# Computing elu+1 with two VectorE operations and one ScalarE operation, and storing and reloading the output accumulator block by block, in a linear-attention and mixture-of-experts kernel

## The reference

```python
x = x + attn(layernorm(x))
x = x + ffn(layernorm(x))

# attn: 16 heads of 64, linear attention
q = elu(q) + 1.0
k = elu(k) + 1.0
kv = einsum('bhnd,bhne->bhde', k, v)
out = einsum('bhnd,bhde->bhne', q, kv) / (q . sum(k) + 1e-8)
out = out @ w_proj + b_proj

# ffn: 8 experts of width 2048, gates by three Sinkhorn rounds, top 2 of 8
g = relu(x @ wg[e]); p = x @ wp[e]
all_out = (g * p) @ wo[e]
return x + sum over the two chosen experts of gate * all_out
```

## Time and profile before

| | us |
|---|---|
| median of 3 timed runs | 8018.8 |
| the three runs | 7903.87, 8018.8, 8377.97 |
| the profiled execution, call | 7267.14 |
| the profiled execution, span of its slowest core | 7265.5 |
| spans of the 8 cores | 7255.6 to 7265.5 |

### The profile page before, as it was taken

How to read it: one execution, slowest core, us unless ns; L and a number is a source line. 1 busy time by engine, 2 the same in 40 slices (tenths; PEclk the granted TensorE clock), 3 DMA queues, 4 the chain that set the end, 5 groups by cost and what they waited for, 6 DMA issues and landing times.

```text
span 7265.5 us, 77246 instructions; the slowest of 8 cores (7255.6 to 7265.5 us)
## 1 busy us (share of the span) xinstructions
PE 6219.6 (86%) x28666; PEld 2747.6 (38%) x29238; DVE 2713.8 (37%) x4957; ACT 977.8 (13%) x1646; POOL 165.5 (2%) x202
## 2 busy tenths in 40 slices
PE   4666655569999999999999996999999999999998
PEld 1222222224444444444444442444444444444443
DVE  2222244443433333333343332333334333333333
ACT  2323311111111111111111110111111111111110
POOL 0000000000000000000000000000000000000000
PEclk8888866679999999999999998999999999999999
DMA  4000011132222222222222224222222222222222
GB/s 73 21 24 18 21 55 55 56 87 35 35 35 35 35 35 40 41 42 36 35 35 35 35 35 110 41 40 42 35 35 35 35 35 35 35 35 35 35 38 62
DMA packets 192672, 298.65 MB, mean 41 GB/s; under 512 B 5930, under 2 KB 137002, under 8 KB 192306
## 3 DMA queue, kind: packets, MB, share of 16 engines
q0 software_dynamic: 169120, 209.75, 19.8%
q1 hardware_dynamic: 23186, 83.93, 3.5%
HBM read 469.84 MB, written 33.55 MB: 69 GB/s over the span
## 4 chain that ended last, share of the span: by engine, by line
PE 68%; DVE 13%; issue 9%; ACT 7%; DMA 2%; DVEq 0%; SPq 0%; ACTq 0%; POOL 0%; POOLq 0%
PE p3p L714 24%; PE p3g L709 24%; PE p3o L754 13%; DVE out_acc L769 8%; PE p1kv L321 2%; PE p2pr L501 2%; ACT rt L726 2%; DVE kb L339 1%; DMA rws<-router_w 1%; PE p2tr L438 1%; ACT qtmp L336 1%; ACT qtmp L384 1%; DVE h2T L442 1%; DVE h1T L309 1%; ACT h1b L296 1%
## 5 line engine op out<-in xcount | busy, mean ns | idle before, releaser
L754 PE MATMUL p3o<-wo_p,t 128*128 128x512 bf16 x8031 | 1841.6, 379 | 333.5 <-DVE out_acc L769 325.5
L709 PE MATMUL p3g<-h2T,wg_p 128*128 128x512 bf16 x8028 | 1923.1, 379 | 9.2 <-DVE sk L628 0.5
L714 PE MATMUL p3p<-h2T,wp_p 128*128 128x512 bf16 x8025 | 1921.6, 379 | 9.0 <-issue 0.2
L736 DVE TENSOR_TENSOR t<-rt,p3p 128x512 bf16<-128x512 f32 x1024 | 704.8, 688 | 3021.3 <-ACT rt L726 3021.2
L769 DVE SCALAR_TENSOR_TENSOR out_acc<-p3o,wsel,out_acc 128x512 f32<-128x512 f32 x2048 | 1482.3, 748 | 483.0 <-PE p3o L754 335.1
L754 PEld LDWEIGHTS p3o<-wo_p,t 128*128 128x128 bf16 x8192 | 783.6, 98 | 1351.5 <-issue 446.1
L726 ACT ACTIVATE rt<-p3g 128x512 f32<-128x512 f32 x1024 | 611.3, 597 | 5047.5 <-PE p3p L714 5047.5
L709 PEld LDWEIGHTS p3g<-h2T,wg_p 128*128 128x128 bf16 x8192 | 802.2, 98 | 968.9 <-issue 7.2
L714 PEld LDWEIGHTS p3p<-h2T,wp_p 128*128 128x128 bf16 x8192 | 802.1, 98 | 968.3 <-issue 5.5
L321 PE MATMUL p1kv<-wqkv_sb,h1T 128*128 128x512 bf16 x992 | 290.4, 442 | 67.6 <-DVE kb L339 39.3
L305 PE MATMUL p1tr<-identb_s,h1b 128*128 128x128 bf16 x256 | 53.4, 262 | 171.5 <-ACT h1b L296 139.5
(11 more groups left out here) (118 smaller groups left out, 1354.8 us busy)
## 6 DMA issues: line engine op xcount, KB each, us to landing
wg_p<-wg POOLq DMA_DIRECT2D x64, 1024.0 KB, 11.3
wp_p<-wp POOLq DMA_DIRECT2D x64, 1024.0 KB, 17.3
wo_p<-wo POOLq DMA_DIRECT2D x64, 1024.0 KB, 21.9
xt<-x SPq DMA_DIRECT2D x64, 512.0 KB, 3.6
base_scr<-xt SPq DMA_DIRECT2D x32, 512.0 KB, 2.6
out_acc<-base_scr SPq DMA_DIRECT2D x32, 512.0 KB, 15.1
out<-out_acc SPq DMA_DIRECT2D x32, 512.0 KB, 7.5
wqkv_sb<-w_qkv POOLq DMA_DIRECT2D x1, 6144.0 KB, 43.2
```

The costliest lines, as they stand in the source:

```text
L709: EM(T, lambda t, b=b, k=k, fsub=fsub, w=w, q=q, it3=it3: t.matmul(p3g[it3 % 2][:], wg_sb[b][:, 512 * k + 128 * fsub:512 * k + 128 * (fsub ...
L714: mmfn = lambda t, b=b, k=k, fsub=fsub, w=w, q=q, it3=it3: t.matmul(p3p[it3 % 2][:], wp_sb[b][:, 512 * k + 128 * fsub:512 * k + 128 * (fsu ...
L736: EM(V, lambda v, qt=qt, fsub=fsub, it3=it3: v.tensor_tensor(t_sb[qt][:, 512 * fsub:512 * (fsub + 1)], rt_sb[it3 % 2][:], p3p[it3 % 2][:], ...
L754: mmfn = lambda t, qt=qt, s4=s4, fsub=fsub, b=b, dmh=dmh: t.matmul(p3o[s4][:], t_sb[qt][:, 512 * fsub + 128 * s4:512 * fsub + 128 * (s4 + 1)],
```

## The change

Three things:

- elu+1 in stage 1, for keys and queries: VectorE writes min(y, 0) from PSUM to `qtmp1` or `qtmp2` in turn, ScalarE takes Exp of it into `qtmp3`, and VectorE computes max(y, 0) + `qtmp3` from PSUM in one operation. VectorE now waits for the matmuls and for the Exp before, ScalarE for the minimum.
- The 16 loads of wave 0 stay ahead of stage 3. Every output block has its own point in the count of additions (`su_done`), noted when the second half of its last addition is emitted. SyncE waits for that point and stores the block.
- In wave 0 it then waits until this store has landed and issues the load of the same block for wave 1. In wave 1 it goes on to the next block.

```diff
             if cc < 2:
-                W(S, SM["kv"])
+                W(V, SM["kv"])
+                W(V, SM["sks"])
+                EM(V, lambda v, pb=pb, cc=cc: v.tensor_single_scalar(
+                    qtmp1[:] if cc == 0 else qtmp2[:], pb[:], 0.0, ALU.min).then_inc(SM["skv"].h, 1))
+                inc(SM["skv"])
+                W(S, SM["skv"])
                 W(S, SM["kvf"])
                 W(S, SM["qf"])
-                EM(S, lambda s, pb=pb: s.activation(qtmp1[:], pb[:], AF.Relu))
-                ssem(lambda s, pb=pb: s.activation(qtmp2[:], pb[:], AF.Relu, scale=-1.0))
-                EM(S, lambda s: s.activation(qtmp3[:], qtmp2[:], AF.Exp, scale=-1.0).then_inc(SM["sks"].h, 1))
+                EM(S, lambda s, cc=cc: s.activation(qtmp3[:],
+                                                    qtmp1[:] if cc == 0 else qtmp2[:],
+                                                    AF.Exp).then_inc(SM["sks"].h, 1))
                 inc(SM["sks"])
                 W(V, SM["sks"])
-                EM(V, lambda v, i=i, cc=cc: v.tensor_tensor(
-                    kb_bf[i % 2][:, 512 * cc:512 * (cc + 1)], qtmp1[:], qtmp3[:],
-                    ALU.add).then_inc(SM["kvf"].h, 1))
+                EM(V, lambda v, pb=pb, i=i, cc=cc: v.scalar_tensor_tensor(
+                    kb_bf[i % 2][:, 512 * cc:512 * (cc + 1)], pb[:], 0.0, qtmp3[:],
+                    ALU.max, ALU.add).then_inc(SM["kvf"].h, 1))
...
-    for w in range(NW):
-        if w > 0:
-            W(SY, SM["st"], 256 * w)
-        W(SY, SM["scf"], scf_hist[-1])
-        W(SY, SM["bst"], bst_hist[-1][0])
-        W(SY, SM["bst1"], bst_hist[-1][1])
-        for su in range(16):
-            dma(SY, out_acc[:, DM * su:DM * (su + 1)],
-                base_d.rearrange("(s p) d -> s p d", p=128)[16 * w + su], SM["bi"])
-        W(SY, SM["o3f"], 32 * NCF * E * (w + 1))
-        for su in range(16):
-            dma(SY, out_d.rearrange("(s p) d -> s p d", p=128)[16 * w + su],
-                out_acc[:, DM * su:DM * (su + 1)], SM["st"])
+    W(SY, SM["scf"], scf_hist[-1])
+    W(SY, SM["bst"], bst_hist[-1][0])
+    W(SY, SM["bst1"], bst_hist[-1][1])
+    for su in range(16):
+        dma(SY, out_acc[:, DM * su:DM * (su + 1)],
+            base_d.rearrange("(s p) d -> s p d", p=128)[su], SM["bi"])
...
                 inc(SM["o3f"])
+                if e == E - 1 and c == NCF - 1 and dmh == 1:
+                    su_done[16 * w + su] = SM["o3f"].v
...
     emitB(NP3 - 1)
+
+    for w in range(NW):
+        for su in range(16):
+            W(SY, SM["o3f"], su_done[16 * w + su])
+            dma(SY, out_d.rearrange("(s p) d -> s p d", p=128)[16 * w + su],
+                out_acc[:, DM * su:DM * (su + 1)], SM["st"])
+            if w == 0:
+                W(SY, SM["st"], SM["st"].v)
+                dma(SY, out_acc[:, DM * su:DM * (su + 1)],
+                    base_d.rearrange("(s p) d -> s p d", p=128)[16 + su], SM["bi"])
```

More of the change, by code:

```diff
@@ L378, in build_program @@
                 inc(SM["q"])
-                W(S, SM["q"])
+                W(V, SM["q"])
+                W(V, SM["sks"])
+                EM(V, lambda v, qi=qi, qc=qc: v.tensor_single_scalar(
+                    qtmp1[:] if qc % 2 == 0 else qtmp2[:], p1q[qi % 2][:], 0.0,
+                    ALU.min).then_inc(SM["skv"].h, 1))
+                inc(SM["skv"])
+                W(S, SM["skv"])
                 W(S, SM["kvf"])
                 W(S, SM["qf"])
-                EM(S, lambda s, qi=qi: s.activation(qtmp1[:], p1q[qi % 2][:], AF.Relu))
-                ssem(lambda s, qi=qi: s.activation(qtmp2[:], p1q[qi % 2][:], AF.Relu, scale=-1.0))
-                EM(S, lambda s: s.activation(qtmp3[:], qtmp2[:], AF.Exp, scale=-1.0).then_inc(SM["sks"].h, 1))
+                EM(S, lambda s, qc=qc: s.activation(qtmp3[:],
+                                                    qtmp1[:] if qc % 2 == 0 else qtmp2[:],
+                                                    AF.Exp).then_inc(SM["sks"].h, 1))
                 inc(SM["sks"])
                 W(V, SM["sks"])
-                EM(V, lambda v, qc=qc, sup=sup: v.tensor_tensor(
+                EM(V, lambda v, qc=qc, sup=sup, qi=qi: v.scalar_tensor_tensor(
                     q_sb[:, NTOK * qc + 512 * sup:NTOK * qc + 512 * (sup + 1)],
-                    qtmp1[:], qtmp3[:], ALU.add).then_inc(SM["qf"].h, 1))
+                    p1q[qi % 2][:], 0.0, qtmp3[:], ALU.max, ALU.add).then_inc(SM["qf"].h, 1))
                 qf_hist.append(inc(SM["qf"]))
@@ L655, in build_program @@
     h2T_done = p2tpf_hist[-1]
+    su_done = {}
     gpf_hist = []
@@ L661, in build_program @@
     w3_hist[0].append(sw3[0].v)
-    for w in range(NW):
-        if w > 0:
-            W(SY, SM["st"], 256 * w)
-        W(SY, SM["scf"], scf_hist[-1])
-        W(SY, SM["bst"], bst_hist[-1][0])
-        W(SY, SM["bst1"], bst_hist[-1][1])
-        for su in range(16):
-            dma(SY, out_acc[:, DM * su:DM * (su + 1)],
-                base_d.rearrange("(s p) d -> s p d", p=128)[16 * w + su], SM["bi"])
-        W(SY, SM["o3f"], 32 * NCF * E * (w + 1))
-        for su in range(16):
-            dma(SY, out_d.rearrange("(s p) d -> s p d", p=128)[16 * w + su],
-                out_acc[:, DM * su:DM * (su + 1)], SM["st"])
+    W(SY, SM["scf"], scf_hist[-1])
[4 more added lines that the diff above has]
+            base_d.rearrange("(s p) d -> s p d", p=128)[su], SM["bi"])
+    SY_DEFERRED = True
     W(T, SM["sktf"], h2T_done)
```

## The result

The changed kernel takes 0.9868 of the time of the one before (95% interval 0.9849 to 0.9888), 1.3% less: all of the interval lies within 2%. The profiled executions differ by 97.5 us: 7265.5 us of span before, 7168.0 after; the forecast was 119.

What follows compares the result with a forecast made beforehand. Most of the span was put on TensorE in the expert stage, untouched; waits in stage 1, between waves and in the tail would yield 48 + 51 + 20 = 119 us, so 8018.8 - 119 = 7900 us, range 7740 to 8050.

Steps and rivals of the forecast that it cites:

- 8018.8 - 119: Whole kernel: the summed gain of 119 us taken off the median of three timed runs, giving 7900 us.
- Part 1, stage 1: Key and query tiles in stage 1: the shorter elu+1 chain gains 48 us (46 to 50).
- the hand-over: Stage 1, VectorE's minimum to ScalarE's Exp: taken as 0.12 us, between 0.10 and 0.15.
- what the chain ends earlier, the next tile starts earlier: Stage 1 key tiles: the second chain's earlier end passes on fully, 0.78 us per 128-token tile, 25 us for 32.
- Part 2, the change of waves: Between the waves: block by block exchange cuts VectorE's stall from 62 to 11 us, gain 51 us (40 to 65).
- the pair: Change of waves: one block's store and load take 3.7 us, so blocks 0 to 11 are exchanged under the matmuls.
- half share: Change of waves: last transfers share DMA engines about equally with the next weights, 11 us becoming 22.
- Part 3, the tail: End of the kernel: only the last four stores remain after the additions, gain 20 us (16 to 21).
- A (slow exchange): Rival at the change of waves: pairs stay slow, wave gain gone at 9.1 us a pair; 7951 us, chance 0.08.
- B: Rival in stage 1: shorter waits keep TensorE's clock up, 61 us more; 180 us in all, 7839 us, chance 0.12.
- C: Rival in the waves: losing the standstill lowers the granted clock, 55 us per 1%; 8180 us at 5%, chance 0.08.
- D (part 1 does nothing): Rival in stage 1: PSUM double buffer binds sooner or the minimum is long; 71 us gain, 7948 us, chance 0.05.

Runs made afterwards that it cites:

- wait_order: Changed kernel with the wait that fires last in stage 1 written behind the long-met ones; ratio 0.9884 (0.9708 to 1.006), cores 0 to 3 span 7142.5 to 7149.4 us.
- stores_only: Changed kernel without the 16 loads for wave 1, SyncE still waiting for every store; stores landed in 2.6 us, no span given.
- spin_old_chain: Kernel before, plus unread TensorE products filling its standstill in stage 1; last query addition starts at 837.4 us, 60.6 us earlier than without them.
- elu_only: New elu+1 chain alone, with the stores and loads of the kernel before; cores 0 to 3 span 7218.0 to 7221.4 us.
- spin_gap_only: Changed kernel with unread TensorE products in the stage 1 standstill only, none between transposes; stage 1 ends at 834.6 us on the slowest core.
- spin: Changed kernel with unread TensorE products in the stage 1 standstill and between transposes; stage 1 ends 72 us earlier, shortest execution 7095.3 us.

## Why the prediction was right or wrong

**The base it was taken from: wrong, and this is the step that failed.** "8018.8 - 119" takes the gain from the median of three timed runs. The prediction saw that this median lay 752 us above the profiled execution, said that no row shows why, and took it all the same. With the full clock on all cores the kernel before takes 7263 to 7268 us, and every longer execution of it whose clocks are on record has a die with a mean of 0.79 to 0.93 in place of 0.94; for the three runs themselves only their length is known. So some 750 us of the 7900 were a lower clock and not the kernel, and the changed kernel at full clock, 7169.6 us, lies 570 us below the lower end of the range. That the plain median of ten executions, 7826, falls within the range is luck: before's is 7706, and by those two the change would have made the kernel slower. The sum against the profiled execution, 7148 us in place of the 7169.6 measured, was the sound part; the number should have been put as that, with the spread as a width. Its 119 us were 97.5, and the two terms below are what was too large.

**Part 1, stage 1: mechanism right, sized 25% too high** (48, measured 38.5). The first mis-sized term is the hand-over. The prediction took 0.12 between 0.10 and 0.15 without asking what made them differ: in the earlier trace rows no wait stands behind the one that fires, in the earlier trace rows one does. After the change two do, and the hand-over is 0.20; wait_order puts it at 0.10 and moves the end by 16 us. The trace of before had this case too, ScalarE's first Relu of a block, with two long-met waits behind the one for TensorE, 0.21 us after TensorE's end at 209.16:

```profile
209.37 0.60 ACT L334 ACTIVATE qtmp<-p1kv 128x512 f32<-128x512 f32 x1 [7.78 <-PE p1kv L325]
```

The second step is "what the chain ends earlier, the next tile starts earlier". That holds only at an unchanged clock: the expected gain for a block, 0.78 us, comes out at 0.55 or 0.72, and at 0.90 or 1.14 with the clock kept. So the change lost to the clock some of what it won; with it kept the whole of part 1 is worth 49.9 us. That this is near the 48 is partly luck: the hand-over of 0.20 is still in it, and the second key tile ends 2.15 us behind the first where the working, read from a block with a late clock, had 2.48. With the short hand-over and the clock as it is, wait_order's stage 1 ends 55 us earlier than that of before, so elsewhere the working was too low; no run takes that apart. (The working also put the fourth tile 0.12 behind the second addition, where the earlier trace rows has 0.15: 0.75 us a block, not 0.78.) The query groups, where the clock is full, came to 2.46 us for 2.9. The duration of both new operations, 0.69 us, and the PSUM buffers as the new bound of every second query tile were right. That the new waits on VectorE cost nothing was right only for what is queued behind them, not for their own time.

**Part 2, the change of waves: mechanism right, sized too high** (51, measured 33.2). Three terms: the pair, 3.7 us forecast and 5.95 measured, since a store beside a load lands in 5.1 and not 2.8 (stores_only: 2.6 without loads); hence, second, block 12 starts 6 us late; and the contended transfers, where "half share" was read from a wg load with a deep queue of stores next to it. The other way round, one store next to a deep queue of weights, it is worse than half: 9.6 and 8.1 us for 2.6 (stores_only), and up to 12.3 with a load beside it too. The measured end lies 43 us behind the last addition, beyond the bound of a third of the engines (36).

**Part 3, the tail: right,** 20.4 for 20.

**Rivals.** A (slow exchange) is half true: 5.95 us a pair over the first twelve, 7.0 over all sixteen, under its point of decision at 9.1. B's price was right to the microsecond (61 forecast, 60.6 by spin_old_chain), but the change didn't bring it about, for the reason given: the standstill ahead of the first tile is untouched. It had to be filled, and the transposes too. C did not happen in the two profiled executions: the granted clock is 1.00 in both waves, before and after. The Trainium skill ("TensorE: Matmul & The Clock Gate", Part 1) has a die fall to 13/16 once three of its cores run dense matmuls; these two traces do not agree, with all four cores of each die in them at 1.00, while core 4 of elu_only's trace had 0.81 from 4800 to 7200 us. D (part 1 does nothing) did not happen. The chances had "within 2%" at 0.67, which it was.

The doubt drawn from the Trainium skill's page "DMA: Bandwidth & Descriptors" (Anatomy of one DMA: about 2 us fixed on each transfer, and so 3.2 us for a lone store as an estimate) was not where the cost lay: alone, a store took 2.6 us here. The page gives that fit for transfers issued from GpSimd; these stores are issued from SyncE. The same page of the Trainium skill has each DMA engine take its queues in turn by packets (Queues, rings and completion order); no run here shows how the engines shared between a store and the weights, only that 2.6 us became 9.6 and 8.1.

## What to carry to other kernels

Cost a transfer with what will be in flight beside it after the change, not by the quietest row of its kind; and before speeding up an exchange, ask whether its last parts are needed at all when the gate asks (a gate for each group was worth 28 us, all the contention included). Write the wait that fires last as the last one: each met wait behind it was 0.05 us here, on every tile of a serial chain. Where TensorE stands still in a loop, price the slow restart first: it cost 61 us here, more than the chain that was being shortened.

## What the runs showed of the hardware

- A hand-over between engines took 0.10, 0.15 and 0.20 us with no, one and two long-met waits behind the one that fires (rows 5; rows 4; the changed kernel's stage 1).
- A 512 KB store from SyncE's queue landed in 2.6 us alone, with TensorE and VectorE at full work (stores_only), 5.1 beside one load of the same size, 9.6 and 8.1 beside three queued weight loads from GpSimd (stores_only), and 12.3 and 11.2 beside those and one load (the changed kernel).
- TensorE at 1.2 GHz, the lower level (granted clock 0.50), ran nine products of a key tile in 4.1 us in place of 2.2. Thirteen products filling the standstill did not keep it at 2.4 GHz in all blocks (spin_gap_only: 17.3 to 20.5 us a block); four more among the eight transposes did in 31 of 32 (spin: 17.2 to 18.0).
